# Routing in a Macaron block: picks from the logits, the second half's scores in the search's rounds, one-hots eight tiles wide

## The reference, cut to what matters

```
probs = softmax(h @ r2_w.T)                      # 4096 tokens x 32 experts
topp, topi = top_k(probs, 2)                     # the two picks of a token, ties to the lower expert
wnorm = topp / topp.sum(-1)
routed = (topi[..., None] == arange(32)).any(1)
score = where(routed, probs, -inf)
idx = argsort(-score, axis=0)[:160].T            # the 160 best tokens of each expert, ties to the lower token
w = weight of the pick, 0 where the token was not routed to that expert
```

## Time and profile before

| | us |
|---|---|
| median of 3 runs | 1924.11 |
| profiled execution, its own time | 1925.8 |
| its span | 1924.1 |
| PE busy in the span | 1540.4 |
| DVE busy | 986.5 |
| ACT busy | 710.7 |
| POOL busy | 569.1 |

### The profile page before, as it was taken

How to read it: one execution, slowest core, us unless ns; L and a number is a source line. 1 busy time by engine, 2 the same in 40 slices (tenths; PEclk the granted TensorE clock), 3 DMA queues, 4 the chain that set the end, 5 groups by cost and what they waited for, 6 DMA issues and landing times. The chain is left out here.

```text
span 1924.1 us, 27153 instructions
## 1 busy us (share of the span) xinstructions
PE 1540.4 (80%) x9510; PEld 1152.9 (60%) x9510; DVE 986.5 (51%) x2826; ACT 710.7 (37%) x1737; POOL 569.1 (30%) x461
## 2 busy tenths in 40 slices
PE   1799979999999577359999986489983569988994
PEld 1656634454544454338989986255551459888893
DVE  5666477777774495864441111256555754521110
ACT  0122227656667276215422222123342425322321
POOL 2444030000000342202445454322210231545336
PEclk9889989999999798558999999699995569999997
DMA  3014273323200022404778784400114026778764
GB/s 96 17 72 129 110 132 68 81 48 76 49 27 2 1 99 80 150 6 145 231 198 229 228 238 81 127 33 29 38 66 159 6 44 194 223 209 240 220 186 55
DMA packets 114068, 212.62 MB, mean 111 GB/s; under 512 B 20149, under 2 KB 79962, under 8 KB 104730
## 3 DMA queue, kind: packets, MB, share of 16 engines
q1 hardware_dynamic: 87066, 178.93, 29.1%
q0 software_dynamic: 26880, 32.13, 11.1%
HBM read 158.71 MB, written 51.90 MB: 109 GB/s over the span
## 5 line engine op out<-in xcount | busy, mean ns | idle before, releaser
L908 DVE TENSOR_REDUCE attnm_top<-psum 128x1 f32<-128x384 f32 (+3 forms) x384 | 215.9, 598 | 67.5 <-PE psum L997 62.5
L1132 ACT ACTIVATE attnm_prob<-psum 128x512 f32<-128x512 f32 (+1 forms) x384 | 192.4, 530 | 129.7 <-PE psum L1007 124.4
L2160 POOL DMA_INDIRECT out<-moe2e_y,moe_scatter_i x80 | 125.6, 1571 | 164.7 <-ACT moe2e_y L2297 99.8
L2160 POOL DMA_INDIRECT x_sum<-moe1e_y,moe_scatter_i x80 | 125.5, 1568 | 156.5 <-ACT moe1e_y L2297 85.9
L2217 PE MATMUL psum<-moe2e_xgT,moe_w_up 128*128 128x160 f32 x1024 | 154.3, 309 | 14.8 <-issue 12.4
L2343 DVE SCALAR_TENSOR_TENSOR moe2e_h<-moe2e_gate,psum 128x160 f32<-128x160 f32 x160 | 50.4, 320 | 218.1 <-ACT moe2e_gate L2270 189.0
L2217 PE MATMUL psum<-moe1e_xgT,moe_w_up 128*128 128x160 f32 x1024 | 151.0, 305 | 8.4 <-issue 5.9
L2217 PEld LDWEIGHTS psum<-moe2e_xgT,moe_w_up 128*128 128x128 f32 x1024 | 147.3, 197 | 17.4 <-issue 16.9
L2343 DVE SCALAR_TENSOR_TENSOR moe1e_h<-moe1e_gate,psum 128x160 f32<-128x160 f32 x160 | 50.2, 321 | 209.2 <-ACT moe1e_gate L2270 185.7
L2217 PEld LDWEIGHTS psum<-moe1e_xgT,moe_w_up 128*128 128x128 f32 x1024 | 144.1, 194 | 10.9 <-issue 10.3
L1300 POOL DMA_INDIRECT moe_xg<-xn_rows,moe_gather_i x80 | 83.5, 1044 | 162.9 <-issue 77.4
(11 more groups left out here) (400 smaller groups left out, 3242.1 us busy)
## 6 DMA issues: line engine op xcount, KB each, us to landing
moe_w_up<-in_expert_up SPq DMA_DIRECT2D x64, 1024.0 KB
moe_w_down<-in_expert_down SPq DMA_DIRECT2D x64, 512.0 KB
attnm_q_hat<-q_parts SPq DMA_DIRECT2D x72, 128.0 KB, 4.7
moe_a_up<-in_adapter_up SPq DMA_DIRECT2D x32, 256.0 KB
q_parts<-attnf_q_part SPq DMA_DIRECT2D x12, 512.0 KB, 2.8
attnm_k_hat<-k_parts SPq DMA_DIRECT2D x72, 64.0 KB, 2.3
x_res<-in_x SPq DMA_DIRECT2D x8, 512.0 KB, 8.6
v_tails<-attnf_v_tail SPq DMA_DIRECT2D x4, 1024.0 KB, 3.9
```

Of the source, the lines that this page charges most:

```text
L908: nc.vector.tensor_reduce(top[:, n // QUADS % 2, tiles[0]:tiles[-1] + 1, hh:hh + 1], s.ps[:, u.bank, 0:len(tiles) * width].rearrange("p (t ...
L1132: nc.scalar.activation(prob[:, i % NPROB, at:GROUP], s.ps[:, u.bank, at:GROUP], ACT.Exp).then_inc(taken[u.bank], 1)
L2160: nc.gpsimd.indirect_dma_start(total, bass.IndirectOffsetOnAxis(ap=scatter_i[:, at:at + 1], axis=0), y[:, q, k, :], None, bounds_check=TOK ...
```

## The change

- In `route`, both picks are taken from the shifted logits (`key`, largest value 0) and no longer from the probabilities; the first pick's test for the largest is `>= 0`, joined with the product with `e_down`; the second pick's largest is searched after the first is set to a very low value. The exponentials go to `prob`, and DVE waits for them after the first pick. The second pick's exponential and that of zero (the first pick's) are taken by ACT from [128 x 32] and [128 x 1] columns.
- A score is now `prob + 4 * missed`, with `missed` 0 or -1, in place of `prob * (pick1 + pick2) - 1 + (pick1 + pick2)`.
- `second.scores` and the shares move into rounds 5 to 13 of the first half's search, one small piece after each round's counts (`beside`); PE's transposes of the second half's scores move behind the eleventh total. The write of the shares to DRAM waits for the last piece.
- The one-hots are one TENSOR_TENSOR comparison for eight tiles (1280 columns), with four tiles innermost (`SIDE`); `place_no` is repeated four times and made by POOL at the start of each `route`; the places (`pos`) become bf16 and are reduced by a maximum. `table` reads every fourth element of a group and waits once for eight tiles. The same functions serve the late half in `experts`.

```
@@ -1172,6 +1172,7 @@
 TWO = [(0, 1), (2, 3), (4,)]
+SIDE, HOTS = 4, 8
...
@@ -1197,7 +1198,7 @@
         at = 0
-        for out, pattern, base, step in ((s.e_down, [[-1, EXPERTS]], EXPERTS, 0), (s.place_no, [[1, CAP]], 1, 0),
+        for out, pattern, base, step in ((s.e_down, [[-1, EXPERTS]], EXPERTS, 0),
...
@@ -1284,8 +1284,9 @@
         self.value = st.sb("value", [P, 2, 2, TILES, VALUES * HALF], BF16)
-        self.hot = st.sb("hot", [P, 2, TILES, CAP], BF16)
-        self.picked = st.sem("picked")
+        self.hot = st.sb("hot", [P, 2, TILES // SIDE, CAP, SIDE], BF16)
+        self.place_no = st.sb("place_no", [P, CAP, SIDE], BF16)
+        self.picked, self.numbered = st.sem("picked"), st.sem("numbered")
...
@@ -1332,7 +1333,7 @@
         self.count, self.base = sb("count", [P, 2]), sb("base", [P, 2])
-        self.pos = sb("pos", [P, 2, TILES])
+        self.pos = sb("pos", [P, 2, TILES], BF16)
...
@@ -1355,12 +1356,12 @@
-    def scores(self, v, key, prob):
-        for g in range(PT):
+    def scores(self, v, missed, prob, groups=range(PT)):
+        for g in groups:
             self.nc.vector.scalar_tensor_tensor(
-                out=self.above[:, g * P:(g + 1) * P].rearrange("p (j e) -> p j e", e=HALF), in0=self.of_half(key)[:, tiles],
-                scalar=-1.0, in1=self.of_half(prob)[:, tiles], op0=ALU.add, op1=ALU.add).then_inc(self.scored, 1)
+                out=self.above[:, g * P:(g + 1) * P].rearrange("p (j e) -> p j e", e=HALF), in0=self.of_half(missed)[:, tiles],
+                scalar=4.0, in1=self.of_half(prob)[:, tiles], op0=ALU.mult, op1=ALU.add).then_inc(self.scored, 1)
...
@@ -1446,13 +1447,17 @@
                                                 mine.rearrange("p (j g) e -> p j g e", j=PARTS), place, ALU.mult))
-        nc.vector.tensor_reduce(self.pos[:, i, :], mine, AX_X, ALU.add).then_inc(self.pos_made, 1)
-    def hots(self, v, i, tiles):
+        nc.vector.tensor_reduce(self.pos[:, i, :], mine, AX_X, ALU.max).then_inc(self.pos_made, 1)
+    def hots(self, v, n):
+        i, t = divmod(n * HOTS, TILES)
+        v.wait_ge(self.m.numbered, 1)
         v.wait_ge(self.pos_made, i + 1)
-        for t in tiles:
-            self.nc.vector.tensor_scalar(self.m.hot[:, i, t], self.s.place_no[:], self.pos[:, i, t:t + 1], None,
-                                         ALU.is_equal).then_inc(self.hot_made, 1)
+        shape = [P, HOTS // SIDE, CAP, SIDE]
+        self.nc.vector.tensor_tensor(
+            self.m.hot[:, i, t // SIDE:(t + HOTS) // SIDE], self.m.place_no[:].rearrange("p (o n) q -> p o n q", o=1).broadcast_to(shape),
+            self.pos[:, i, t:t + HOTS].rearrange("p (b o q) -> p b o q", o=1, q=SIDE).broadcast_to(shape),
+            ALU.is_equal).then_inc(self.hot_made, 1)
...
@@ -1558,14 +1563,16 @@
-    def table(self, pe, i, tiles):
+    def table(self, pe, k):
         pe.wait_ge(self.pos_made, 2)
+        pe.wait_ge(self.hot_made, k + 1)
         last = 2 * TILES - 1
-        for t in tiles:
-            n, rows = i * TILES + t, slice(t % 4 * VALUES * HALF, (t % 4 + 1) * VALUES * HALF)
-            pe.wait_ge(self.hot_made, n + 1)
-            ins = self.nc.tensor.matmul(self.s.ps[rows, self.bank, 0:CAP], self.m.value[:, i, self.half, t], self.m.hot[:, i, t],
-                                        start=(n < 4), stop=(n > last - 4), skip_group_check=True)
+        for n in range(k * HOTS, (k + 1) * HOTS):
+            i, t = divmod(n, TILES)
+            rows = slice(t % 4 * VALUES * HALF, (t % 4 + 1) * VALUES * HALF)
+            ins = self.nc.tensor.matmul(self.s.ps[rows, self.bank, 0:CAP], self.m.value[:, i, self.half, t],
+                                        self.m.hot[:, i, t // SIDE, :, t % SIDE], start=(n < 4), stop=(n > last - 4),
+                                        skip_group_check=True)
...
@@ -1925,9 +1932,12 @@
     key = sb("key", [P, TILES, EXPERTS])
+    ints = sb("ints", [P, CAP], I32)
+    zero, unit = sb("zero", [P, 1]), sb("unit", [P, 1])
     share = sb("share", [P, TILES, ROW - C])
-    dve, shifted, exped, shared, shares_out, cleared = (sem(n) for n in ("dve", "shifted", "exped", "shared", "shares_out", "cleared"))
+    dve, shifted, exped, zeroed, second_best, shared, shares_out, cleared, counted = (
+        sem(n) for n in ("dve", "shifted", "exped", "zeroed", "second_best", "shared", "shares_out", "cleared", "counted"))
...
@@ -1943,7 +1953,11 @@
         def _(pool):
+            nc.gpsimd.iota(ints[:], [[1, CAP]], base=1, channel_multiplier=0).then_inc(counted, 1)
             nc.gpsimd.memset(share[:], 0.0).then_inc(cleared, 1)
+            pool.wait_ge(counted, 1)
+            nc.gpsimd.tensor_copy(m.place_no[:], ints[:].rearrange("p (n o) -> p n o", o=1).broadcast_to(
+                [P, CAP, SIDE])).then_inc(m.numbered, 1)
...
@@ -1955,7 +1969,11 @@
             act.wait_ge(shifted, 1)
-            nc.scalar.activation(prob[:], prob[:], ACT.Exp).then_inc(exped, 1)
+            nc.scalar.activation(prob[:], key[:], ACT.Exp).then_inc(exped, 1)
+            act.wait_ge(zeroed, 1)
+            nc.scalar.activation(unit[:], zero[:], ACT.Exp)
+            act.wait_ge(second_best, 1)
+            nc.scalar.activation(col[:, 3, :], col[:, 2, :], ACT.Exp).then_inc(exped, 1)
...
@@ -1966,13 +1984,14 @@
             first.turn_scores(pe)
-            second.turn_scores(pe)
                 first.total(pe, k, True)
+                if k == 10:
+                    second.turn_scores(pe)
             first.turn_places(pe)
-            for i in range(2):
-                first.table(pe, i, range(TILES))
+            for k in range(2 * TILES // HOTS):
+                first.table(pe, k)
...
@@ -1983,47 +2002,55 @@
-            top, total, m1, m2, k1 = (col[:, i, :] for i in range(5))
+            top, total, best2, exp2, k1, m1, m2 = (col[:, i, :] for i in range(7))
+            down = s.e_down[:].rearrange("p (o e) -> p o e", o=1).broadcast_to([P, TILES, EXPERTS])
+            nc.vector.memset(zero[:], 0.0).then_inc(zeroed, 1)
             chain.link(nc.vector.tensor_reduce(top, prob[:], AX_X, ALU.max))
-            nc.vector.tensor_tensor(prob[:], prob[:], per_expert(top), ALU.subtract).then_inc(shifted, 1)
+            nc.vector.tensor_tensor(key[:], prob[:], per_expert(top), ALU.subtract).then_inc(shifted, 1)
+            v.wait_ge(shifted, 1)
+            chain.link(nc.vector.scalar_tensor_tensor(out=pick1[:], in0=key[:], scalar=0.0, in1=down, op0=ALU.is_ge, op1=ALU.mult))
+            chain.link(nc.vector.tensor_reduce(k1, pick1[:], AX_X, ALU.max))
+            chain.link(nc.vector.tensor_tensor(pick1[:], pick1[:], per_expert(k1), ALU.is_equal))
             v.wait_ge(exped, 1)
+            chain.link(nc.vector.scalar_tensor_tensor(out=key[:], in0=pick1[:], scalar=MASKED, in1=key[:], op0=ALU.mult, op1=ALU.add))
+            nc.vector.tensor_reduce(best2, key[:], AX_X, ALU.max).then_inc(second_best, 1)
+            v.wait_ge(second_best, 1)
+            chain.link(nc.vector.tensor_tensor(pick2[:], key[:], per_expert(best2), ALU.is_equal))
+            chain.link(nc.vector.tensor_tensor(pick2[:], pick2[:], down, ALU.mult))
+            chain.link(nc.vector.tensor_reduce(k1, pick2[:], AX_X, ALU.max))
+            nc.vector.tensor_tensor(pick2[:], pick2[:], per_expert(k1), ALU.is_equal).then_inc(m.picked, 1)
             chain.link(nc.vector.reciprocal(total, total))
+            v.wait_ge(m.picked, 1)
+            nc.vector.scalar_tensor_tensor(out=key[:], in0=pick1[:], scalar=-1.0, in1=pick2[:], op0=ALU.add, op1=ALU.add)
             chain.link(nc.vector.tensor_tensor(prob[:], prob[:], per_expert(total), ALU.mult))
-            def pick(src, best, out):
-                down = s.e_down[:].rearrange("p (o e) -> p o e", o=1).broadcast_to([P, TILES, EXPERTS])
-                chain.link(nc.vector.tensor_reduce(best, src[:], AX_X, ALU.max))
-                chain.link(nc.vector.tensor_tensor(out[:], src[:], per_expert(best), ALU.is_equal))
-                chain.link(nc.vector.tensor_tensor(out[:], out[:], down, ALU.mult))
-                chain.link(nc.vector.tensor_reduce(k1, out[:], AX_X, ALU.max))
-                return nc.vector.tensor_tensor(out[:], out[:], per_expert(k1), ALU.is_equal)
-            chain.link(pick(prob, m1, pick1))
-            chain.link(nc.vector.scalar_tensor_tensor(out=key[:], in0=pick1[:], scalar=-2.0, in1=prob[:], op0=ALU.mult,
-                                                      op1=ALU.add))
-            pick(key, m2, pick2).then_inc(m.picked, 1)
-            v.wait_ge(m.picked, 1)
-            chain.link(nc.vector.tensor_tensor(key[:], pick1[:], pick2[:], ALU.add))
-            chain.link(nc.vector.tensor_tensor(prob[:], prob[:], key[:], ALU.mult))
             first.scores(v, key, prob)
-            second.scores(v, key, prob)
-            chain.link(nc.vector.tensor_tensor(total, m1, m2, ALU.add))
-            chain.link(nc.vector.reciprocal(total, total))
```

(22 more changed lines are left out.)

14 lines of the change are left out of this document (6 added, 8 removed).

## The result

The changed kernel takes a median of 1906.2 us in 20 runs (1896.36 to 1919.15). The kernel before took 1921.51 us in 20 runs (1908.05 to 1930.14). The ratio is 0.9921, 95% interval 0.9907 to 0.9936: 15.3 us faster by the medians, 12.3 to 17.9 us by the interval. The forecast was 1905.7 us, from a sum of 18.4 us. That the two times lie 0.5 us apart is luck in part: the forecast started from a median of three runs, 1924.11 us, which the twenty runs put at 1921.51 us, and the gain is 3.1 us smaller than the sum. The two errors nearly cancel; what can be judged is the gain.

A forecast was written before the change was run, and what follows sets the result against it. Serial routing stages, one chain from first instruction to first gather, stand before PE-bound experts. Per stage 5.0 + 4.5 - 0.3 = 9.2 us, twice 18.4 us, from 1924.1 to 1905.7 us; range 1900.5 to 1914 us.

The forecast's parts named there:

- Picks: Start of each routing stage: fewer DVE instructions and no wait for the exponentials bring scores 5.0 us earlier a stage.
- The moved scores and shares: Second half's scores and shares, moved from before the search into its rounds' DVE waits: 0 us, bound 0 to 2.6.
- Transposes: PE's four transposes behind the eleventh total exceed PE's spare time in a search round: 0.3 us lost once a stage.
- round of 2.75 us: Expected sign in the search: rounds 6 to 14 still 2.45 us long, but for one of 2.75 us.
- One-hots: End of each routing stage: eight wide DVE comparisons at 0.74 us each start the table's copy 4.5 us earlier.
- Rival 1: Wide one-hots run at one element a cycle, 1.40 us each; gain 3.95 us a stage, time 1916.2 us; chance 0.12.
- The late half: Second half's one-hots in the experts, where PE never stops for them: 0 us, bounds -1 and +1 us a layer.
- rival 3: Table matmuls reading every fourth bf16 element slow PE: +8.9 us a layer, 1941.9 us; chance 0.04.
- No clock term: At the experts' start PE is at half clock before and after, so the forecast adds nothing for clock.
- The sum: Both routing stages: 5.0 + 4.5 - 0.3 = 9.2 us each, 18.4 us in all, to 1905.7 us.
- Rival 2: Moved work doesn't fit the search rounds and lands on the chain: gain 5.75 us a stage, 1912.6 us; chance 0.09.
- Rival 4: Experts wait for their weights and give the gain back: no change, 1924.1 us; chance 0.03.

The follow-up runs named there:

- The kernels that take the first term away: Changed kernel with two tiles innermost in the one-hots, 0.9909; the same also without the second wait in four late rounds, 0.9906.
- the two kernels of part 3: Changed kernel with second half's scores, transposes and shares back before the search, 1903.56 us; changed kernel with share pieces' waits moved to the next piece, 1903.81 us.
- the two kernels with 36 and 42 fillers: Changed kernel plus 36 unread PE matmuls after the turned table, 0.988; with 42, two tiles innermost and no second wait in late rounds, 0.9887.

## Why the prediction was right, and where it was off

- **Picks, 5.0 us a stage: right.** 17.74 us to the scores (forecast 17.8), 5.11 us less than before. In the kernel with the picks alone 4.7 and 4.9 us of it reach the stages, as the new shares cost 0.3 us there (3.04 us to the halves for 2.72). The two unwaited steps are 1.14 us apart (783.19 to 784.33 us), as worked out.
- **The moved scores and shares, 0 us: right.** DVE stands idle for 1.83 us in their old place, and the halves start 2.74 us after the scores for 2.72 us before. The new shares would have cost 0.3 us in front of the search, which the prediction didn't count; the move hides it.
- **Transposes, 0.3 us: right size, wrong cause.** The rounds lost 0.36 us a stage, but by the chain's second wait in front of four decisions. The prediction said that a late round has room for the moved work on DVE, which held; it looked at what each piece takes and not at what waiting for it adds. No round of 2.75 us appeared, and a kernel with the transposes and without the second waits has rounds of 2.45 us.
- **One-hots, 0.74 us each, 4.5 us a stage: right.** The copy of the table starts 6.61 us after the first (forecast 6.8), 4.74 us gained; 0.30 us of it goes again behind the copy, by the clock. In the kernel with the one-hots alone 4.4 and 4.6 us reach the stages. The rule weighed there (the Trainium skill, "Vector Engine (DVE) Microarchitecture Reference", section 5.1, Performance modes) agrees on both its sides: 0.74 us with two, four or eight tiles innermost, 1.40 us with one element read over and over. Rival 1 is what the kernel with the tile outermost does: with the same comparison and types, the layout alone makes 0.74 or 1.40 us.
- **The late half, 0 us: the step that was off.** DVE's side cost nothing, as it has time there. On PE eight table matmuls take 0.39 us for 0.25, which is +1.1 us a layer, 2.2 us in all. That is rival 3 in small: 0.049 us a matmul where 0.031 us passed, far under the 0.09 us from which it decides. The bound of 1 us a layer was set from DVE's durations and just missed it. The prediction weighed the note on SBUF cachelines of "SBUF — State Buffer" in the Trainium skill, by which a step of four 2-byte elements is free; the measurement differs (0.39 against 0.25 us) and decides.
- **"No clock term": wrong by a little.** Inside the stage the shorter row of table matmuls no longer gave PE full clock, and turning the table took 0.30 us longer in the first layer. In the experts the first 32 up matmuls of the first layer took 7.39 us for 6.25, 1.1 us lost in this pair of profiles; the second layer lost none. The prediction took half clock at the experts' start before and after as a reason for no difference; at what time the clock comes back differs from layer to layer and from kernel to kernel (6.2 to 7.6 us for the same 32), so the 1.1 us are not shown to be the change's.
- **The sum.** Stages -9.1 and -9.4 us against the forecast of -9.2. Less 2.2 us for the matmuls that is -16.3 us, and -15.2 us with the 1.1 us of clock; the medians say -15.3, the interval -12.3 to -17.9, so the forecast of 18.4 us lies a little outside. The kernels that take the first term away are at 0.9909 and 0.9906, 17.5 and 18.1 us under the kernel before. But the two kernels of part 3, which keep it, are at 0.9901 and 0.9904. The intervals reach 3 to 5.5 us to either side, so the times can't tell whether the sum closes; the stages' lengths and the 0.39 us are shown.
- **Rival 2** is out with the 1.83 us of idle DVE and the rounds with moved work in them, of which none takes more than 2.54 us.
- **Rival 4** is out: the experts did not take the 18.5 us back, they took 693.8 us before and 691.9 us after, and the kernel is 15.3 us faster. PE's unexplained idle time in front of the up matmuls of the second layer fell from 12.4 to 8.4 us.

Open: why the stalls in the experts were shorter in the two kernels with 36 and 42 fillers, and what decides whether the clock survives a gap. Each row of the table of stalls rests on one profile, and the experts of kernels without fillers spread over 11 us there (683.5 to 694.8).

## What to carry to other kernels

When a result is laid out anew so that its producer runs at two elements a cycle, price its consumer at that step too, on the engine that sets the pace: here the smallest inner row that gave DVE its speed, two, was also one that PE read at almost no cost (0.26 us for 0.25). Work put into a loop's waits costs what its own wait adds to the loop's next step, even where it fits. Idle time in a serial stage in front of PE-bound work has a price behind it, in clock; but read it over a whole layer and over several executions. The same holds inside the stage: making a dense row of matmuls shorter can take the full clock from what follows it, here 0.3 us.
